# Dividing the softmax probabilities of a local-attention kernel on two engines instead of one

## The chip, the cores and the metric

One core of a Trainium2 chip. The metric is the device time of one execution in microseconds (us). Engines are named TensorE (PE in the profile, PEld for its weight loads), VectorE (DVE), ScalarE (ACT), GpSimd (POOL) and SyncE (SP, which only issues transfers).

## The reference, cut to what matters

The input x has shape (4, 2048, 256), float32. First comes a full self-attention without weights over each sequence of 2048 rows, then two layers of a transformer block, with layer norms and residuals around both parts. The change lies in the two layers. Each layer computes, per row, queries, keys and values for 8 heads of 64, normalises and rotates queries and keys, and attends within windows of 128 rows to the own window and the one before:

```python
sim = jnp.einsum('bhwid,bhwjd->bhwij', bq, bk)      # 128 x 256 for each head and window
sim = jnp.where(mask, -jnp.finfo(sim.dtype).max, sim)
attn = jax.nn.softmax(sim, axis=-1)                 # exp(sim - max) / row sum
out = jnp.einsum('bhwij,bhwjd->bhwid', attn, bv)
...
x = x + o @ wo
h = shift_token(x)                                  # then layer norm
h = h @ w1 + b1
a, g = jnp.split(h, 2, axis=-1)
h = a * jax.nn.gelu(g, approximate=False)
x = x + h @ w2 + b2
```

The division by the row sum in `softmax` is the operation that the change moves.

## The kernel before, in words

The program has a first part (`phase_a`, the unweighted attention, up to some 790 us), a preparation of the weights, and the second part (`phase_b`, both layers, from some 820 us to the end). Only the second part is touched.

**Slots.** The second part is a hand-written software pipeline over 128 windows (64 for each layer) of 128 rows. `slots` (lines 481 to 497) calls a function `run(s, r, pairs, layer)` once for each slot s, with r = s % 4; every engine has its own `run`, and each engine works through its own list in the written order, held only by semaphores. In slot s the projections of window s are made, the attention of window s - 1 up to the probabilities, the rest of the attention of window s - 2, and the layer norm of window s - 3. The feed-forward part works on pairs of windows: its first product (w1) and the gelus come at the end of the even slots (r = 0 and 2), its second product (w2) in the odd slots (r = 1 and 3). So there are 64 slots of each kind that hold attention work. The first 8 slots of each layer are written out; the others run in a loop (`Fori`) with four slots to a turn, and the last slots are written out again. `t` in the code is the window that a block of lines treats.

**The softmax, and who does what around it.** For window t = s - 1, in slot s:

- TensorE makes the scores of a pair of heads p (lines 909 to 915), four pairs, into four PSUM banks.
- VectorE adds the mask, scales, and keeps each head's 128 x 256 scores in SBUF in `probs`, with the negated maximum in `negmax` (line 1160).
- ScalarE takes the exponential in place and gives the row sum (line 1021), eight instructions; then `keep_hT` copies the transposed input of the next window out of PSUM (line 971, to `hT_hi`).
- VectorE, in `normalise(p)` (lines 1166 to 1173), waits for the exponentials of the pair, takes the reciprocal of the two row sums (line 1170, `rinv`) and multiplies both heads' probabilities by it in place (line 1173). Between the pairs stand two other steps: `normalise(0)`, `normalise(1)`, the residual add (line 1184), `normalise(2)`, `keep_hT` (line 1047, the low part `hT_lo`, which waits for ScalarE's `hT_hi`), `normalise(3)` (lines 1175 to 1188).
- In the next slot TensorE transposes the probabilities (line 886) after a wait on `probs_ready`, and ScalarE copies them out of PSUM (line 1009).

**What stands behind it on the two queues.** On VectorE: in odd slots of layer 1 the output norm (line 1105), in even slots six instructions `hid` (line 1196), each after its gelu; then the next slot begins with the low parts of the queries and keys (lines 1120 and 1123, `qT_lo`, `kT_lo`), which wait for ScalarE's `qT_hi` and `kT_hi`. On ScalarE: in even slots a table load and six gelus (line 1036), each into one of two buffers `gl`, so that the third waits for the first `hid` and so on; then the next slot begins with the copies of queries and keys out of PSUM (lines 987, 991, 994), the squares (998, 1000), the values (1003), the transposed probabilities (1009), the attention output (1012), and `h2T` (979) ahead of the next exponentials. On TensorE: in the odd slot behind an even one the transposes of the keys (line 855) wait for the third `hid` (line 853), since they write to the same bank, the projections (line 870) for the first two, and the projection of the values for `qT_lo` (line 863); the transposes of the probabilities (line 886) in even slots wait for the add of line 1084 on VectorE (`xpp_ready`, line 878).

```python
normalise(0)
normalise(1)
...
nc.vector.tensor_tensor(xp[:, r % 2, :], ps[:, 2, 0:D], xr[:, r % 2, :], ALU.add).then_inc(xp_ready, 1)
normalise(2)
if in_range(s + 1):
    keep_hT(s + 1)
normalise(3)
```

Of the kernel before, what the change touches and what calls it, by code (L numbers as in the profile page):

```python
# [21 lines left out]
ALU = mybir.AluOpType  # L22
ACT = mybir.ActivationFunctionType
# [9 lines left out]
LAYERS, HEADS, DH = 2, 8, 64  # L33
INNER = HEADS * DH
HP = HEADS // 2
# [28 lines left out]
def wait(eng, sem, count):  # L64

    if not (isinstance(count, int) and count <= 0):
        eng.wait_ge(sem, count)
# [408 lines left out]
def in_range(t):  # L476

    return not isinstance(t, int) or 0 <= t < NT
# [21 lines left out]
def phase_b(nc, w, consts, x2_dram, xs_dram, xp_dram, rot_dram, out):  # L500
# [9 lines left out]
    with ExitStack() as keep:  # L510
        def sb(name, shape, dt=F32):
            return keep.enter_context(nc.sbuf_tensor("b_" + name, shape, dt))
# [16 lines left out]
        with ExitStack() as ctx:  # L529
# [3 lines left out]
            def sem(name):  # L533
                return ctx.enter_context(nc.semaphore("p_" + name))
# [148 lines left out]
        with ExitStack() as ctx:  # L683
# [22 lines left out]
            probs = sb("probs", [P, HEADS, 2 * P])  # L706
            rowsum, rinv = sb("rowsum", [P, HEADS]), sb("rinv", [P, HEADS])
# [28 lines left out]
            kT_both = sem("kT_both")  # L736
            scores_done, mask_ready = sem("scores_done"), sem("mask_ready")
            scores_kept, exp_done = sem("scores_kept"), sem("exp_done")
            rinv_ready, probs_ready = sem("rinv_ready"), sem("probs_ready")
            pT_done, pT_kept = sem("pT_done"), sem("pT_kept")  # L740
            pv_done, oT_hi, oT_lo, wo_done, xp_ready, xb_ready = (sem(n) for n in ("pv_done", "oT_hi", "oT_lo", "wo_done", "xp_ready", "xb_ready"))
            st2_ready, mv2_ready, var2_ready, rstd2_ready = (sem(n) for n in ("st2_ready", "mv2_ready", "var2_ready", "rstd2_ready"))
# [75 lines left out]
            def _(pe):  # L818
# [21 lines left out]
                def run(s, r, pairs, layer):  # L840
                    t = s - 1
# [32 lines left out]
                    t = s - 2  # L874
                    if in_range(t):

                        if r % 2 == 0:
                            wait(pe, xpp_ready, s - 4)
                        else:
                            wait(pe, hid_ready, HC * (pairs - 1))  # L880
                        for p in range(HP):
                            if p == HP - 1 and in_range(s - 1):
                                pe.wait_ge(kT_lo, 2 * s)
                            pe.wait_ge(probs_ready, HEADS * t + 2 * p + 2)
                            for n in range(4):
                                last = nc.tensor.transpose(ps[:, 3 + p, n * P:(n + 1) * P],  # L886
                                                           probs[:, 2 * p + n // 2, (n % 2) * P:(n % 2 + 1) * P], ident_f[:])
                            last.then_inc(pT_done, 1)

                        pe.wait_ge(v_kept, t + 1)  # L890
                        if not in_range(s):
                            pe.wait_ge(h2T_kept, s - 3)
                        for p in range(HP):
                            pe.wait_ge(pT_kept, HP * t + p + 1)
                            for c in range(2):
                                window = (r - 2 - (r + c) % 2) % 4
                                for h in range(2):
                                    last = nc.tensor.matmul(ps[h * DH:(h + 1) * DH, 7, p * P:(p + 1) * P],  # L898
                                                            v[:, window, (2 * p + h) * DH:(2 * p + h + 1) * DH],
                                                            probsT[:, p, (2 * h + c) * P:(2 * h + c + 1) * P],  # L900
                                                            start=(c == 0), stop=(c == 1))
                        last.then_inc(pv_done, 1)
                    t = s - 1
# [13 lines left out]
                    t = s - 2  # L917
# [44 lines left out]

                transpose_hx(0, 0)
                slots(pe, run)

            @block.scalar
            def _(act):
                def keep_hT(t):
                    act.wait_ge(hT_done, t + 1)
                    wait(act, k_done, t)  # L970
                    nc.scalar.copy(hT_hi[:], ps[:, 7, 0:D].rearrange("p (k n) -> p k n", k=KD)).then_inc(hT_hi_kept, 1)
# [9 lines left out]
                def run(s, r, pairs, layer):  # L981
                    t = s - 1
# [21 lines left out]
                    t = s - 2  # L1004
# [8 lines left out]
                    t = s - 1  # L1013
# [10 lines left out]
                        keep_h2T(s - 3, r, pairs)  # L1024
                    if in_range(s + 1):
                        keep_hT(s + 1)
                    j = pairs - 2
                    if r % 2 == 0 and in_range(2 * j):
                        for c, bank in enumerate(W1_BANKS):
# [9 lines left out]
                keep_hT(0)  # L1039
                act.wait_ge(vk_cleared, 4)  # L1040
                slots(act, run)

            @block.vector
            def _(dve):
# [68 lines left out]
                def run(s, r, pairs, layer):  # L1113
                    t = s - 1
# [11 lines left out]
                    t = s - 3  # L1126
# [9 lines left out]
                    t = s - 3  # L1136
# [10 lines left out]
                    t = s - 1  # L1147
# [18 lines left out]
                    def normalise(p):  # L1166
                        t = s - 1
                        if in_range(t):
                            dve.wait_ge(exp_done, HEADS * t + 2 * p + 2)
                            nc.vector.reciprocal(rinv[:, 2 * p:2 * p + 2], rowsum[:, 2 * p:2 * p + 2]).then_inc(rinv_ready, 1)  # L1170
                            dve.wait_ge(rinv_ready, HP * t + p + 1)
                            for h in range(2 * p, 2 * p + 2):
                                nc.vector.tensor_scalar(probs[:, h, :], probs[:, h, :], rinv[:, h:h + 1], None, ALU.mult).then_inc(probs_ready, 1)  # L1173

                    normalise(0)
                    normalise(1)
                    t = s - 2
                    if in_range(t):
# [4 lines left out]
                        wait(dve, xb_ready, t - 1)  # L1183
# [4 lines that stand above are left out]
# [82 lines left out]
def build(nc, x, wqkv, q_scale, k_scale, wo, ln_g, ln_b, w1, b1, w2, b2, ident, rot, mask, out):  # L1270
    x2_dram = nc.dram_tensor("x2_dram", [NW * P, D], F32).ap()
    xs_dram = nc.dram_tensor("xs_dram", [STREAM_BLOCKS * P, D], F32).ap()
    xp_dram = nc.dram_tensor("xp_dram", [STREAM_BLOCKS * P, D], F32).ap()
    rot_dram = nc.dram_tensor("rot_dram", [P, LAYERS * WPB, 4 * DH], F32).ap()
    phase_a(nc, x, ident, x2_dram, xs_dram, xp_dram)
    weights = dict(wqkv=wqkv, q_scale=q_scale, k_scale=k_scale, wo=wo, ln_g=ln_g, ln_b=ln_b, w1=w1, b1=b1, w2=w2, b2=b2)
    phase_b(nc, weights, dict(ident=ident, rot=rot, mask=mask), x2_dram, xs_dram, xp_dram, rot_dram, out)
# [49 lines left out]
```

## Time and profile before

| | us |
|---|---|
| median of 3 runs | 3440.58 (3440.16 to 3442.09) |
| span of the profiled execution | 3440.9 |
| VectorE busy | 2975.0 (86%) |
| ScalarE busy | 2315.4 (67%) |
| TensorE matmul busy | 3200.0 (93%) |
| GpSimd busy | 1876.9 (55%) |

The span of the profiled execution runs from its first to its last instruction; no other time of that execution is given, and the span lies 0.3 above the median of the runs. Busy shares are means over the whole span; the rows that are quoted further down come from single slots. A row of a view in order of time gives the start in us from the span's start, the length in us, the engine, the line, the operation and how often it stands there in a row; in brackets the idle time ahead of it and who ended it.

### The profile page before, as it was taken

Reading aid. Unit: us, or ns where it says so; the run is one execution under the profiler, and the core shown is the slowest. Engines: PE = TensorE matmul, PEld = TensorE weight load, DVE = VectorE, ACT = ScalarE, POOL = GpSimd, SP = SyncE. Lnnn points to the kernel's source line nnn. Section 1 sums busy time; section 2 is a strip of 40 time slices with the busy share of each in tenths; the row PEclk is TensorE's granted clock in tenths of the full one; section 3 lists DMA queues with packets and bytes.
Section 4 is the critical chain, followed back from the end, with each engine's and each line's share of the span. In section 5 each row is a group of like instructions: output and inputs, shape, how many; then the busy total and the mean of one; then the engine's idle time right before and its main releaser. Section 6 shows DMA issues by size and latency. Waiting matters only on the chain.

```text
span 3440.9 us, 85961 instructions
## 1 busy us (share of the span) xinstructions
PE 3200.0 (93%) x24600; PEld 2670.4 (78%) x24600; DVE 2975.0 (86%) x8121; ACT 2315.4 (67%) x5021; POOL 1876.9 (55%) x2307
## 2 busy tenths in 40 slices
PE   6999999973999999999999999999999999999997
PEld 3666667672888888888888888888888888888886
DVE  6888787857899989988989989998998999899995
ACT  5435353503787777777777777877777777777774
POOL 2433333335665655655655656666665566666662
PEclk9999999985999999999999999999999999999999
DMA  1111111134111111111111111111111111111111
GB/s 35 46 52 41 56 37 55 40 119 140 35 43 40 37 40 41 41 41 41 37 40 45 37 45 38 41 55 43 43 45 46 46 43 43 44 45 51 46 45 36
DMA packets 205536, 163.08 MB, mean 47 GB/s; under 512 B 25646, under 2 KB 203282, under 8 KB 204946
## 3 DMA queue, kind: packets, MB, share of 16 engines
q1 hardware_dynamic: 205330, 161.06, 15.3%
q14 instruction: 166, 1.36, 0.1%
q8 instruction: 40, 0.66, 0.1%
HBM read 106.44 MB, written 54.54 MB: 47 GB/s over the span
## 4 chain that ended last, share of the span: by engine, by line
DVE 24%; issue 18%; PE 18%; ACT 12%; POOL 1%; DVEq 1%; ACTq 1%; DMA 0%; SPq 0%; POOLq 0%
PE b_ps L898 4%; DVE b_probs L1173 4%; PE b_ps L948 3%; ACT b_probs L1021 3%; PE b_ps L870 2%; DVE b_kT_low L1123 2%; DVE b_probs L1160 2%; ACT b_gl L1036 2%; ACT L1021 2%; PE b_ps L886 2%; DVE b_qT L1120 2%; PE b_ps L913 2%; PE b_ps L914 2%; DVE b_t L1062 2%; ACT b_qT L987 2%
## 5 line engine op out<-in xcount | busy, mean ns | idle before, releaser
L870 PE MATMUL b_ps<-b_wqkv,b_hT_hi 128*128 128x512 f32 x1536 | 503.4, 409 | 43.2 <-DVE b_qT L1120 42.2
L1222 POOL TENSOR_TENSOR b_rstd<-b_var,b_mhalf 128x1 f32<-128x1 f32 x128 | 72.2, 564 | 821.1 <-DVE b_var L1134 821.1
L1021 ACT ACTIVATE b_probs<-b_probs,b_negmax 128x256 f32<-128x256 f32 x1024 | 505.6, 495 | 5.7 <-DVE b_negmax L1160 3.3
L948 PE MATMUL b_ps<-b_h2T,b_w 128*128 128x256 f16 x4224 | 474.2, 273 | 0.7 <-ACT b_h2T L979 0.7
L948 PEld LDWEIGHTS b_ps<-b_h2T,b_w 128*128 128x128 f16 x4224 | 414.5, 98 | 49.3 <-ACT b_h2T L979 0.9
L1212 POOL TENSOR_TENSOR b_sq<-b_sq 128x512 f32<-128x512 f32 (+5 forms) x768 | 418.1, 544 | 58.2 <-ACT b_sq L1000 17.9
L1173 DVE TENSOR_SCALAR b_probs<-b_probs,b_rinv 128x256 f32<-128x256 f32 x1024 | 424.8, 456 | 18.1
L1244 POOL TENSOR_TENSOR b_rn<-b_ss_min,b_mhalf 128x16 f32<-128x16 f32 x128 | 379.2, 2963 | 34.9 <-DVE b_ss_min L1071 33.3
L870 PEld LDWEIGHTS b_ps<-b_wqkv,b_hT_hi 128*128 128x128 f32 x1536 | 281.0, 193 | 114.8 <-DVE b_qT L1120 57.8
L442 PE MATMUL a_ps<-a_xs,a_E 128*128 128x256 f16 x3072 | 345.2, 273 | 4.1 <-POOL a_xs L233 4.0
L959 PE MATMUL b_ps<-b_w,b_hid 128*128 128x256 f32 x1536 | 342.2, 379 | 1.2 <-DVE b_hid L1196 1.2
L434 PE MATMUL a_ps<-a_xnT 128*128 128x512 f16 x1536 | 338.0, 384 | 3.0 <-ACT a_xnT L382 2.4
L442 PEld LDWEIGHTS a_ps<-a_xs,a_E 128*128 (+1 forms) x3072 | 297.8, 98 | 40.0 <-issue 6.6
L1160 DVE CUSTOM_DVE_ANT_0 b_probs<-b_ps,b_mask,b_rn 128x256 f32<-128x256 f32 x768 | 323.6, 474 | 0.0
L959 PEld LDWEIGHTS b_ps<-b_w,b_hid 128*128 128x128 f32 x1536 | 286.8, 190 | 37.9 <-DVE b_hid L1196 1.5
L870 PE MATMUL b_ps<-b_wqkv,b_hT_lo 128*128 128x512 f32 x768 | 307.2, 400 | 0.0
L434 PEld LDWEIGHTS a_ps<-a_xnT 128*128 x1536 | 151.3, 99 | 188.5 <-issue 11.5
L1009 ACT COPY b_probsT<-b_ps 128x512 f32<-128x512 f32 x512 | 266.0, 619 | 26.8 <-PE b_ps L886 26.4
L886 PEld LDWEIGHTS b_ps<-b_ident_f,b_probs 128*128 128x128 f32 x2048 | 233.9, 144 | 56.3 <-DVE b_xpp L1084 23.1
L898 PE MATMUL b_ps<-b_probsT,b_v 128*64 128x128 f32 x4096 | 261.0, 280 | 17.2 <-ACT b_probsT L1009 17.1
L886 PE MATMUL b_ps<-b_ident_f,b_probs 128*128 128x128 f32 x2048 | 253.9, 278 | 24.9 <-DVE b_xpp L1084 23.5
L898 PEld LDWEIGHTS b_ps<-b_probsT,b_v 128*64 128x64 f32 x4096 | 217.5, 136 | 55.4 <-ACT b_probsT L1009 36.6
(136 smaller groups left out, 7305.4 us busy)
## 6 DMA issues: line engine op xcount, KB each, us to landing
b_hx<-xs_dram SPq DMA_DIRECT2D x256, 64.0 KB, 1.9
b_rot<-rot_dram SPq DMA_DIRECT2D x128, 128.0 KB, 2.1
b_xr<-xs_dram SPq DMA_DIRECT2D x128, 128.0 KB, 2.1
xp_dram<-b_xp SPq DMA_DIRECT2D x128, 128.0 KB, 1.7
b_h<-xp_dram SPq DMA_DIRECT2D x256, 64.0 KB, 1.8
a_xn<-in_L_attn_x_dram SPq DMA_DIRECT2D x20, 512.0 KB, 3.8
a_x_res<-in_L_attn_x_dram SPq DMA_DIRECT2D x66, 128.0 KB, 2.1
x_dram<-a_x SPq DMA_DIRECT2D x64, 128.0 KB, 1.7
```

What stands on the lines that cost most here:

```text
L434: last = nc.tensor.matmul(ps[:, 4 * u + n, :], xnT[:, a, k, rows], xnT[:, c, k, n * 512:(n + 1) * 512], start=(k == 0 and a == 0 and c == ...
L442: last = nc.tensor.matmul(ps[:, bank, 0:D], E[:, a, j, ds(i * P, P)], xs[:, c, j, :], start=(j == 0 and a == 0 and c == 0), stop=(j == WPB ...
L870: last = nc.tensor.matmul(ps[:, bank, :], hT[:, k, :], wqkv[:, ds(layer(s), 1), part, k, bank * INNER:(bank + 1) * INNER], start=(k == 0 a ...
L886: last = nc.tensor.transpose(ps[:, 3 + p, n * P:(n + 1) * P], probs[:, 2 * p + n // 2, (n % 2) * P:(n % 2 + 1) * P], ident_f[:])
L898: last = nc.tensor.matmul(ps[h * DH:(h + 1) * DH, 7, p * P:(p + 1) * P], v[:, window, (2 * p + h) * DH:(2 * p + h + 1) * DH], probsT[:, p, ...
L948: last = nc.tensor.matmul(ps[:, bank, half * 2 * P:(half + 1) * 2 * P], w1[:, ds(layer(2 * j), 1), wp, k, first:first + P], h2T[:, hp, k, ...
L959: last = nc.tensor.matmul(ps[:, 3, n * D:(n + 1) * D], hid[:, c, n * P:(n + 1) * P], w2[:, ds(layer(2 * j), 1), c, :], start=(c == 0), sto ...
L1021: nc.scalar.activation(probs[:, h, :], probs[:, h, :], ACT.Exp, bias=negmax[:, h:h + 1], scale=-1.0, accum_out=rowsum[:, h:h + 1]).then_in ...
L1160: nc.vector.tensor_tensor_reduce(probs[:, h, :], ps[:, 3 + p, (h % 2) * 2 * P:(h % 2 + 1) * 2 * P], which, rn[:, (r - 1) % 2, h:h + 1], AB ...
L1173: nc.vector.tensor_scalar(probs[:, h, :], probs[:, h, :], rinv[:, h:h + 1], None, ALU.mult).then_inc(probs_ready, 1)
L1212: nc.gpsimd.tensor_tensor(target, target, sq[:, :, width:2 * width], ALU.add).then_inc(ss_halved, 1)
L1244: nc.gpsimd.tensor_tensor(rn[:, r % 2, :], ss_min[:], mhalf[:], ALU.pow).then_inc(rn_ready, 1)
```

## The change

The reciprocals of all four pairs stay on VectorE. The multiplications of pairs 0 and 1 stay there too; those of pairs 2 and 3, four instructions in each slot, become ScalarE activations with the function Copy and the reciprocal as a per-partition scale, placed behind `keep_hT` and ahead of the gelus. TensorE waits for the first two pairs on `probs_ready` and for the other two on a new semaphore `probs_divided`.

```diff
-            rinv_ready, probs_ready = sem("rinv_ready"), sem("probs_ready")
+            rinv_ready, probs_ready, probs_divided = sem("rinv_ready"), sem("probs_ready"), sem("probs_divided")
...
-                            pe.wait_ge(probs_ready, HEADS * t + 2 * p + 2)
+                            if p < HP // 2:
+                                pe.wait_ge(probs_ready, HEADS // 2 * t + 2 * p + 2)
+                            else:
+                                pe.wait_ge(probs_divided, HEADS // 2 * t + 2 * p + 2 - HEADS // 2)
...
                     if in_range(s + 1):
                         keep_hT(s + 1)
+                    t = s - 1
+                    if in_range(t):
+                        for p in range(HP // 2, HP):
+                            act.wait_ge(rinv_ready, HP * t + p + 1)
+                            for h in range(2 * p, 2 * p + 2):
+                                nc.scalar.activation(probs[:, h, :], probs[:, h, :], ACT.Copy, scale=rinv[:, h:h + 1]).then_inc(probs_divided, 1)
                     j = pairs - 2
                     if r % 2 == 0 and in_range(2 * j):
...
-                            for h in range(2 * p, 2 * p + 2):
-                                nc.vector.tensor_scalar(probs[:, h, :], probs[:, h, :], rinv[:, h:h + 1], None, ALU.mult).then_inc(probs_ready, 1)
+                            if p < HP // 2:
+                                for h in range(2 * p, 2 * p + 2):
+                                    nc.vector.tensor_scalar(probs[:, h, :], probs[:, h, :], rinv[:, h:h + 1], None, ALU.mult).then_inc(probs_ready, 1)
```

## Rows read from the trace of the kernel before

**Rows 1.** the page: busy us (share of the span) of each engine
```profile
PE 3200.0 (93%) x24600; PEld 2670.4 (78%) x24600; DVE 2975.0 (86%) x8121; ACT 2315.4 (67%) x5021; POOL 1876.9 (55%) x2307
```

**Rows 2.** slot r = 2, layer 0: window; length; busy PE, PEld, DVE, ACT, POOL; clock; DMA
```profile
1170.22:1190.89 20.67, 20.67 (x179) 18.46 (x179) 19.32 (x55) 16.87 (x40) 11.63 (x13) 1.00 0.19 59
```

**Rows 3.** ScalarE in order of time, end of slot r = 2, layer 0
```profile
1184.70 0.35 ACT L971 CAST b_hT_hi<-b_ps 128x256 fp32r<-128x256 f32 x1
1185.07 1.28 ACT L1036 ACT_TABLE_LOAD   x1
1186.36 1.02 ACT L1036 ACTIVATE b_gl<-b_ps,b_b,b_w_unit 128x256 f32<-128x256 f32 x2
...
1190.28 1.19 ACT L987 CAST b_qT<-b_ps 64x512 fp32r<-64x512 f32 x2
```

**Rows 4.** VectorE in order of time, the same stretch
```profile
1184.79 0.15 DVE L1170 RECIPROCAL b_rinv<-b_rowsum 128x2 f32<-128x2 f32 x1
...
1186.04 1.36 DVE L1173 TENSOR_SCALAR b_probs<-b_probs,b_rinv 128x256 f32<-128x256 f32 x2
1187.31 0.87 DVE L1196 SCALAR_TENSOR_TENSOR b_hid<-b_ps,b_b1a,b_gl 128x256 f32<-128x256 f32 x2
...
1190.89 1.41 DVE L1120 TENSOR_TENSOR b_qT<-b_ps,b_qT 64x512 fp32r<-64x512 f32 x2
```

**Rows 5.** GpSimd in order of time, the same stretch
```profile
1185.46 1.04 POOL L1249 TENSOR_TENSOR b_kr<-b_t,b_rn 128x512 f32<-128x512 f32 x1
```

**Rows 6.** TensorE in order of time, the slot behind it
```profile
1196.09 2.13 PE L898 MATMUL b_ps<-b_probsT,b_v 128*64 128x128 f32 x32 [0.33 <-ACT b_probsT L1009]
```

**Rows 7.** groups by line and shape, ScalarE, whole span: busy us, mean ns
```profile
L1021 ACT ACTIVATE b_probs<-b_probs,b_negmax 128x256 f32<-128x256 f32 x1024 | 505.6, 495 | 5.7 <-DVE b_negmax L1160 3.3
...
L1036 ACT ACTIVATE b_gl<-b_ps,b_b,b_w_unit 128x256 f32<-128x256 f32 x320 | 167.2, 562 | 46.5 <-DVE b_hid L1196 30.6 <-PE b_ps L948 14.0
...
L641 ACT ACTIVATE b_w<-b_w,b_w_unit 128x1536 f32<-128x1536 f32 x2 | 3.0, 1560 | 0.0
```

**Rows 8.** ScalarE in order of time, end of a slot r = 0, layer 1
```profile
2334.21 1.02 ACT L1036 ACTIVATE b_gl<-b_ps,b_b,b_w_unit 128x256 f32<-128x256 f32 x2
...
2337.78 1.19 ACT L987 CAST b_qT<-b_ps 64x512 fp32r<-64x512 f32 x2
```

**Rows 9.** ScalarE in order of time, end of slot r = 1, layer 0
```profile
1168.10 0.35 ACT L971 CAST b_hT_hi<-b_ps 128x256 fp32r<-128x256 f32 x1
1169.56 1.19 ACT L987 CAST b_qT<-b_ps 64x512 fp32r<-64x512 f32 x2 [1.10 <-PE b_ps L848]
```

**Rows 10.** VectorE in order of time, the same stretch
```profile
1167.52 1.62 DVE L1173 TENSOR_SCALAR b_probs<-b_probs,b_rinv 128x256 f32<-128x256 f32 x2
1169.06 0.41 DVE L1047 TENSOR_TENSOR b_hT_lo<-b_ps,b_hT_hi 128x256 fp32r<-128x256 f32 x1
...
1169.58 0.62 DVE L1173 TENSOR_SCALAR b_probs<-b_probs,b_rinv 128x256 f32<-128x256 f32 x2
1170.22 1.41 DVE L1120 TENSOR_TENSOR b_qT<-b_ps,b_qT 64x512 fp32r<-64x512 f32 x2
```

**Rows 11.** ScalarE in order of time, end of an odd slot, layer 1
```profile
2232.38 0.35 ACT L971 CAST b_hT_hi<-b_ps 128x256 fp32r<-128x256 f32 x1
2233.93 1.19 ACT L987 CAST b_qT<-b_ps 64x512 fp32r<-64x512 f32 x2 [1.20 <-PE b_ps L848]
```

**Rows 12.** VectorE in order of time, the same stretch
```profile
2234.44 0.73 DVE L1105 TENSOR_SCALAR b_fin<-b_xpp,b_mvf,b_rstdf 128x256 f32<-128x256 f32 x2
2235.20 1.41 DVE L1120 TENSOR_TENSOR b_qT<-b_ps,b_qT 64x512 fp32r<-64x512 f32 x2
```

**Rows 13.** VectorE in order of time, at a turn of the loop, layer 0, then layer 1
```profile
1211.06 1.41 DVE L1120 TENSOR_TENSOR b_qT<-b_ps,b_qT 64x512 fp32r<-64x512 f32 x2 [2.47 <-issue]
...
2317.01 1.41 DVE L1120 TENSOR_TENSOR b_qT<-b_ps,b_qT 64x512 fp32r<-64x512 f32 x2 [2.42 <-issue]
```

**Rows 14.** waits of VectorE, whole span: us in total, times, longest
```profile
DVE b_qT L1120 <- issue: 61.4, 25, 2.9
```

## The prediction

> **What bounds the kernel now.** I read the page first. VectorE is busy 86% of the span, ScalarE 67% [rows 1], which invites moving work from the one to the other. That share is a mean, so I went on to the instructions in order of time at the ends of single slots. The slot r = 2 of layer 0 shows TensorE with matmuls on record in all of its 20.67 us, VectorE in 19.32, ScalarE in 16.87 [rows 2]: there is no single bound, and what counts is which engine is late where the slots join. The joint is ScalarE's copy of the queries (line 987), on which VectorE's line 1120 waits.
>
> In an **even** slot ScalarE runs from the last exponentials over the copy of line 971, the table load and six gelus to line 987 [rows 3]. Nothing lies idle ahead of the load (1184.70 + 0.35 = 1185.05, load at 1185.07). VectorE takes its first `hid` at 1187.31 [rows 4], although the first gelu ends at about 1186.36 + 0.56 = 1186.92: there VectorE is late, by 0.4. So both queues are close to critical, and ScalarE has 0.35 to spare: from first gelu to line 987 it takes 3.92 here (1186.36 to 1190.28) [rows 3] and 3.57 in the slot whose `hid` come in time [rows 8].
>
> In an **odd** slot ScalarE idles 1.10 to 1.20 ahead of line 987, released by TensorE [rows 9, 11]. VectorE's line 1120 starts 0.66 behind line 987 in layer 0 (1169.56 to 1170.22) [rows 9, 10], just behind the first of its two halves, so VectorE is no later than TensorE. In layer 1 VectorE has the output norm besides and starts 1.27 behind (2233.93 to 2235.20) [rows 11, 12]: there it is the late one.
>
> **The price of a division on ScalarE.** No row shows it at this size. Line 641 is the same operation (Copy, scale from a column, in place) on 1536 columns, 1.560 us; the exponential, with one column operand, takes 0.495 on 256 [rows 7]. The line through both has 0.83 ns a column, so the two are of one kind and a division takes 0.495. Two gelus of 0.562 take 1.02 together [rows 3, 7], so they start 0.46 apart, 0.10 less than their length; divisions then start 0.40 apart. Four push the next instruction back by 1.60 where it may overlap, and by 3 x 0.40 + 0.495 = 1.70 where it does not, as the table load. Bounds: line 971's 0.35 [rows 3], 0.25 apart, and the gelu's 0.562, 0.46 apart. I take 0.40, since line 641 is the very operation.
>
> **Removed on VectorE.** In an odd slot pair 2 takes 1.54 (1167.52 to 1169.06) and pair 3 0.53, together 2.07 [rows 10]. In an even slot pair 3 takes 1.27 (1186.04 to 1187.31) [rows 4], and pair 2, which nothing disturbs there, 0.53: 1.80. The reciprocals stay.
>
> **Even slots, 64.** The reciprocal of pair 2 is ready at 1184.94 [rows 4], before ScalarE is free, and that of pair 3 follows `hT_lo` at about 1185.6; no wait. The divisions start at 1185.07, the load moves by 1.71 to 1186.78, the first gelu to 1188.07. VectorE is now free long before, so from there the 3.57 hold: line 987 at 1191.64 instead of 1190.28, 1.36 later, and line 1120 with it. VectorE's 1.80 turn into waiting for the first gelu. Where the 3.57 hold already, in the slots r = 0 behind a turn of layer 1's loop (12), it is the full 1.71. Sum 52 x 1.36 + 12 x 1.71 = 91.2. It is not made good in the odd slot: TensorE waits there for the third `hid`, and 0.33 for ScalarE's copy of the probabilities [rows 6], so the delay passes on to the next exponentials.
>
> **Odd slots.** Layer 0: the divisions start at 1168.10 + 0.37 = 1168.47, line 987 can start at 1170.07, against 1169.56 [rows 9]: 0.51 later, line 1120 too, VectorE's 2.07 worth nothing. VectorE's reciprocal of pair 3 is ready at about 1168.97 (`hT_lo` needs line 971, 1168.45, then 0.34 and 0.15), before the third division. There are 32 such slots, 13 of them ahead of a turn of the loop; 19 x 0.51 = 9.7. Layer 1: line 987 at 2232.75 + 1.60 = 2234.35, line 1120 some 0.61 behind, at 2234.96 instead of 2235.20 [rows 11, 12]; VectorE would be ready at 2234.05. 20 x (-0.24) = -4.8.
>
> **Turns of the loop, 25** [rows 14], 13 in layer 0 and 12 in layer 1. Ahead of line 1120 VectorE stands for 2.47 or 2.42 without a releaser [rows 13]; I take it for the cost of the jump back. It starts when VectorE's last instruction is through, and that one ends 1.2 earlier (1170.20 to 1168.97 in the measure of rows 10; in layer 1 1.15). If ScalarE pays nothing at its own jump, the gain is -1.2 and -1.15. If it pays as VectorE does behind its last division, layer 0 has 1168.47 + 1.70 + 2.47 + 0.61 = 1173.25 against 1172.69, +0.56, and layer 1 -0.1. No row shows ScalarE's jump on its own, since TensorE holds it back at that place. I take the middle: 13 x (-0.3) - 12 x 0.65 = -12; ends -29 and +6.
>
> **The sum.** 91.2 + 9.7 - 4.8 - 12 = 84 us. The span is 3440.9 and the median 3440.58, so both are one base: 3440.6 + 84 = 3525.
>
> **Semaphores and queues.** No transfer moves. ScalarE's new wait stands ahead of gelus and of line 987; it is met each time, as shown, because the reciprocals stay in VectorE's order ahead of `hid`. TensorE's wait for `probs_divided` comes late in the next slot, over 4 us behind the last division.
>
> **The rivals.**
> *VectorE is the bound (faster).* Its place is VectorE's queue between line 1170 and line 1120. If ScalarE's divisions fell into idle time, each pair of slots would lose 1.80 + 2.07 = 3.87, or 64 x 3.87 = 248 in all: 3193. For it: the 86%; and pair 3 takes 1.36 instead of 0.62 while GpSimd works on SBUF (1185.46 for 1.04) [rows 4, 5]. Against: no idle time of ScalarE between line 971 and the gelus [rows 3]. It decides as soon as the gelus can slip by 1.36 without moving line 987. The Trainium skill's Perfetto Trace Analysis, section Optimizing Scalar/DVE Operations, says that with VectorE saturated it may pay to give work to ScalarE, and that VectorE and GpSimd share a port; by that rule this rival holds. The slowed pair agrees with the port, the missing idle time speaks against the rule here.
> *Cheap divisions.* At 0.25 apart each slot has 0.60 less: even slots 91.2 - 38.4 = 53, odd slots of layer 0 nothing, of layer 1 20 x (-0.66) = -13 (TensorE then holds line 987 at 2233.93), turns -29: +11, 3451.
> *Dear divisions, or a slower clock.* At 0.46 apart each slot has 0.24 more: 91.2 + 15.4 + 9.7 + 4.6 + 13 x 0.80 + 1 = 132, 3573. TensorE also waits about 1 us more in each even slot; its granted clock is 1.00 there [rows 2], the 2.4 GHz level, and if it fell at times, the time would be in this region too.
> *The freed time of the odd slots and turns just cancels the even ones:* needs both low ends and more; within 0.2%.
>
> The Trainium skill's ScalarE: Activation LUTs, section Rules for kernel authors, wants multiplications on VectorE and not on ScalarE. The undisturbed pair of 0.62 on VectorE [rows 10] against 0.40 + 0.495 for a pair on ScalarE agrees with it.
>
> **Chances and range.** Forecast 0.74; VectorE bound 0.06; cheap 0.07; dear or slower clock 0.10; cancelled 0.03. A measurement of this kernel can tell about 0.2%, some 7 us, from no change. Only the first rival is faster, only the last is within 0.2%: faster 0.06, same 0.03, slower 0.91. The forecast's own ends are the turns' (3508 and 3543), and half the way to the cheap and dear prices widens them to 3475 and 3570, which leaves out less than 2 in 10.
>
> **What would show it.** In the changed profile: four Copy instructions of 0.49 in each slot, 0.40 apart, 512 in all; in even slots the table load 1.7 later behind line 971, VectorE idle some 2.6 us ahead of its first `hid`, released by the gelu, and 3.57 from first gelu to line 987; in odd slots no idle time of ScalarE ahead of line 987; VectorE's busy share down by some 240 us of work, ScalarE's up by 250. At the turns, an idle time of ScalarE ahead of line 987 without a releaser, or none, settles that term. Wrong would be: a gap between line 971 and the first division (the reciprocal late), line 987 of the even slots less than 1 us later, or TensorE's clock below 1.00 in layer 0.

## The result, and the profile after

| | us |
|---|---|
| before, 4 runs | 3441.04 median (3440.16 to 3442.09) |
| after, 4 runs | 3486.75 median (3484.45 to 3490.2) |
| ratio | 1.0134, 95% interval 1.0120 to 1.0148 |
| span of the profiled execution after | 3484.5 |

The kernel is slower, by 46 us: on the side that the prediction gave, inside its range of 3475 to 3570, and 38 us short of its +84.

The page of after, busy us of each engine (before: [rows 1]):

```profile
PE 3208.2 (92%) x24600; PEld 2657.2 (76%) x24600; DVE 2734.9 (78%) x7609; ACT 2510.3 (72%) x5533; POOL 1868.4 (54%) x2307
```

VectorE's busy time fell by 240 us, ScalarE's rose by 195 (not by 250 as predicted: 512 divisions of 0.499 are 255, but busy time counts an overlap of neighbours once: the row below has 218.3 for them), and TensorE's stayed. The time rose all the same.

Groups by line and shape, ScalarE in after: busy us, mean ns, idle time ahead of them and its releasers. The divisions are line 1035; lines 971, 987, 1036, 1047, 1120, 1170, 1173 and 1196 of before are now 974, 990, 1045, 1056, 1129, 1179, 1183 and 1206.

```profile
L1024 ACT ACTIVATE b_probs<-b_probs,b_negmax 128x256 f32<-128x256 f32 x1024 | 505.6, 495 | 5.7 <-DVE b_negmax L1169 3.3
...
L1035 ACT ACTIVATE b_probs<-b_probs,b_rinv 128x256 f32<-128x256 f32 x512 | 218.3, 499 | 1.1 <-DVE b_rinv L1179 1.1
```

There are 512 divisions of 0.499, as long as an exponential (0.495), and they wait 1.1 us in all.

ScalarE in order of time, end of an even slot of layer 0 in after (before: [rows 3]):

```profile
1155.41 0.35 ACT L974 CAST b_hT_hi<-b_ps 128x256 fp32r<-128x256 f32 x1
1155.67 1.71 ACT L1035 ACTIVATE b_probs<-b_probs,b_rinv 128x256 f32<-128x256 f32 x4
1157.39 1.28 ACT L1045 ACT_TABLE_LOAD   x1
1158.69 1.02 ACT L1045 ACTIVATE b_gl<-b_ps,b_b,b_w_unit 128x256 f32<-128x256 f32 x2
...
1162.26 1.19 ACT L990 CAST b_qT<-b_ps 64x512 fp32r<-64x512 f32 x2
```

Four divisions last 1.71, so they stand 0.40 apart. From line 974 to the table load it is 1.98 against 0.37 before, so the load comes 1.61 later; from line 974 to the copy of the queries it is 6.85 against 5.58 [rows 3], so the copy comes 1.27 later. The 3.57 from the first gelu to that copy is what [rows 8] had.

VectorE in order of time at the same place (before: [rows 4]):

```profile
1156.14 0.15 DVE L1179 RECIPROCAL b_rinv<-b_rowsum 128x2 f32<-128x2 f32 x1
1159.29 0.94 DVE L1206 SCALAR_TENSOR_TENSOR b_hid<-b_ps,b_b1a,b_gl 128x256 f32<-128x256 f32 x2 [2.99 <-ACT b_gl L1045]
```

VectorE is through with the slot's softmax at 1156.29 and waits 2.99 us for the first gelu. Its freed time has become waiting.

TensorE's clock in two even slots of layer 0, by window: length; busy PE, PEld, DVE, ACT, POOL; granted clock; DMA (before: [rows 2]):

```profile
1140.20:1162.20 22.00, 19.64 (x171) 16.99 (x170) 17.13 (x50) 17.33 (x41) 11.57 (x13) 1.00 0.19 57
1180.96:1202.94 21.98, 20.75 (x178) 18.19 (x177) 17.60 (x52) 18.57 (x44) 11.56 (x13) 1.00 0.22 66
```

The slot is 1.3 longer at a granted clock of 1.00, the 2.4 GHz level, as before: the clock has no part in what the divisions cost here. It has a part at the turns of layer 1, further down.

ScalarE in order of time, end of an odd slot of layer 0 in after (before: [rows 9]):

```profile
1178.48 0.35 ACT L974 CAST b_hT_hi<-b_ps 128x256 fp32r<-128x256 f32 x1
1178.74 1.71 ACT L1035 ACTIVATE b_probs<-b_probs,b_rinv 128x256 f32<-128x256 f32 x4
1180.35 1.17 ACT L990 CAST b_qT<-b_ps 64x512 fp32r<-64x512 f32 x2
```

Here the idle time ahead of the copy of the queries, 1.10 before, is filled, and 0.41 more: 1.87 from line 974 to it against 1.46.

Waits of after, whole span: us in total, times, longest.

```profile
DVE b_hid L1206 <- ACT b_gl L1045: 232.0, 197, 5.6
...
DVE b_hT_lo L1056 <- ACT b_hT_hi L974: 75.0, 106, 3.7
DVE b_qT L1129 <- ACT b_qT L990: 73.7, 58, 3.1
```

And two waits of before:

```profile
DVE b_hid L1196 <- ACT b_gl L1036: 47.1, 141, 5.6
ACT b_qT L987 <- PE b_ps L848: 72.6, 64, 2.5
```

In after, ScalarE's wait for TensorE at line 990 (line 987 of before) is down from 72.6 us to a single one of 2.5. ScalarE is now the late one at the joints of two slots.

So far it is much as predicted. The difference lies at the **turns of the loop**. VectorE in order of time at a turn of layer 0, then at one of layer 1, in after (before: [rows 13]):

```profile
1219.25 0.15 DVE L1179 RECIPROCAL b_rinv<-b_rowsum 128x2 f32<-128x2 f32 x1
1222.44 1.41 DVE L1129 TENSOR_TENSOR b_qT<-b_ps,b_qT 64x512 fp32r<-64x512 f32 x2 [3.04 <-ACT b_qT L990]
...
2320.11 0.73 DVE L1114 TENSOR_SCALAR b_fin<-b_xpp,b_mvf,b_rstdf 128x256 f32<-128x256 f32 x2 [0.22 <-DVE b_rinv L1179]
2321.47 1.41 DVE L1129 TENSOR_TENSOR b_qT<-b_ps,b_qT 64x512 fp32r<-64x512 f32 x2 [0.62 <-ACT b_qT L990]
```

The first of them names ScalarE's copy as the releaser. ScalarE in order of time at the same turn says otherwise:

```profile
1220.38 1.18 ACT L990 CAST b_qT<-b_ps 64x512 fp32r<-64x512 f32 x2
```

The first half of that copy, which is all that line 1129 needs, ended about 0.6 later, at 1221.0, and VectorE still stood for 1.4 us. The idle time is the stall of the jump back, now mostly hidden behind a wait. In layer 1 the stall is gone altogether: line 1129 starts 0.6 behind ScalarE's copy (line 990 at 2320.87), as inside the loop. Where did it go?

The DMA view of 2300 to 3200 us (layer 1), rows of the queues, has an answer to look into: a queue that carries instructions. Its packets, in before and then in after:

```profile
q14 instruction: 55, 0.45, 0.2%
```

```profile
q14 instruction: 5, 0.04, 0.0%
```

Before has 5 packets of 8 KB to each of its 11 turns in this stretch; in after they are gone but for 5 and 3 others on another queue, all outside of 2400 to 3200. In 1100 to 1900 us (layer 0) both have 50, again 5 to a turn.

The whole account by kind of slot follows. A slot's length is taken from one copy of the queries on ScalarE to the next in order of time; each figure is the mean over the loop's rounds (14 in layer 0, 13 in layer 1), and r = 0 is the slot that begins a round. The first round is entered without a jump back, so there are 13 and 12 jumps, the turns that the prediction counts. "Shifted" kernels are explained with their experiments.

| kernel | layer 0: r = 0, 1, 2, 3 | layer 1: r = 0, 1, 2, 3 |
|---|---|---|
| before | 23.07, 17.68, 20.71, 17.67 | 23.83, 18.29, 21.41, 18.29 |
| after | 23.47, 18.08, 21.98, 18.08 | 21.98, 18.71, 21.98, 18.70 |
| even slots only | 24.26, 17.67, 22.03, 17.68 | 25.64, 18.30, 22.76, 18.30 |
| odd slots only | 22.09, 18.08, 20.81, 18.08 | 23.80, 18.69, 20.63, 18.70 |
| behind the gelus | 23.63, 17.95, 22.08, 17.95 | 22.09, 18.71, 22.09, 18.69 |
| after, shifted | 21.99, 18.08, 21.98, 18.08 | 21.97, 18.69, 21.97, 18.69 |
| before, shifted | 20.68, 17.67, 20.69, 17.68 | 21.40, 18.32, 21.41, 18.29 |
| before, shifted less | 20.68, 17.69, 20.69, 17.68 | 23.69, 18.31, 21.40, 18.29 |
| after, stalling in layer 1 | 23.48, 18.09, 21.99, 18.09 | 23.70, 18.70, 21.98, 18.70 |
| odd, pair 2 alone, shifted | 20.65, 17.68, 20.65, 17.67 | 20.78, 18.33, 20.77, 18.29 |
| odd, pairs 2 and 3, shifted | 20.64, 18.08, 20.64, 18.09 | 20.63, 18.81, 20.64, 18.69 |
| even, pair 3 alone, shifted | 22.26, 17.68, 22.22, 17.66 | 22.96, 18.33, 22.96, 18.30 |
| even, pair 2 alone, shifted | 21.22, 17.69, 21.20, 17.68 | 21.95, 18.33, 21.95, 18.29 |

Both r = 0 and r = 2 are even slots, so their difference is what a turn costs, as a mean over all rounds: before 2.36 in layer 0 and 2.42 in layer 1, after 1.49 and nothing. In us: before 14 x 2.36 + 13 x 2.42 = 65, after 14 x 1.49 = 21. The turns gave back 44.

In layer 1 a part of this is TensorE's clock. Two turns of before and one of after, from one copy of the queries to the next (columns as above):

```profile
2313.24:2337.78 24.54, 22.27 (x178) 19.25 (x177) 19.99 (x59) 17.32 (x40) 13.23 (x15) 0.93 0.20 59
2560.33:2583.87 23.54, 21.17 (x180) 18.37 (x179) 20.14 (x59) 17.12 (x39) 13.26 (x15) 1.00 0.20 60
```

```profile
2361.51:2383.47 21.96, 20.71 (x178) 18.17 (x177) 17.11 (x50) 18.56 (x44) 13.21 (x15) 1.00 0.24 71
```

In before, 8 of the 12 slots behind a jump in layer 1 have a granted clock of 0.93 on average; they last 24.26 us, the other four 23.60. In after all are at 1.00. So some 8 x 0.66 = 5 of the 31 us that the turns of layer 1 cost before go with the clock. In this loop of before every slot without a jump ahead of it is at 1.00.

### The profile page after: what moved, and what is told of

It reads as the page before. It is cut to its first block, busy times and chain, and to the rows that moved or that the text cites. A ratio compares the mean times of both kernels' runs of the same rounds, so it can differ in the third digit from the quotient of the medians.

```text
span 3484.5 us, 85882 instructions
## 1 busy us (share of the span) xinstructions
PE 3208.2 (92%) x24600; PEld 2657.2 (76%) x24600; DVE 2734.9 (78%) x7609; ACT 2510.3 (72%) x5533; POOL 1868.4 (54%) x2307
## 4 chain that ended last, share of the span: by engine, by line
ACT 27%; PE 20%; issue 15%; DVE 12%; POOL 1%; ACTq 1%; DVEq 0%; DMA 0%; POOLq 0%; SPq 0%
ACT b_probs L1024 10%; PE b_ps L901 6%; ACT b_probs L1035 4%; PE b_ps L889 4%; PE b_ps L916 3%; ACT b_gl L1045 3%; PE b_ps L917 3%; DVE b_kT_low L1132 2%; ACT b_qT L990 2%; ACT L1045 2%; PE b_ps L962 2%; DVE b_qT L1129 2%; DVE b_hid L1206 2%; ACT L1024 2%; DVE b_xpp L1093 1%
## 5 line engine op out<-in xcount | busy, mean ns | idle before, releaser
L1206 DVE SCALAR_TENSOR_TENSOR b_hid<-b_ps,b_b1a,b_gl 128x256 f32<-128x256 f32 (+1 forms) x384 | 181.2, 482 | 238.4 <-ACT b_gl L1045 232.0
L382 ACT COPY a_xnT<-a_ps 128x512 f16 x80 | 46.1, 587 | 310.3 <-PE a_ps L412 310.2
```

## The experiments

The theory: the divisions move ScalarE's copy of the queries back in each even slot, VectorE's freed time is worthless, and the turns of the loop gave back more than predicted. Rivals: the even slots cost less than their 1.3, or the loss comes from TensorE's wait for the third `hid` (it waits 56.0 us there in all in after) and not from ScalarE's queue.

### The move in one kind of slot alone

A pair that a list `ON_ACT` names is divided by ScalarE, the others by VectorE; its first entry is for odd slots, its second for even ones. It is `((), (2, 3))` in the kernel with the move in even slots only and `((2, 3), ())` in the other. TensorE's counts on the two semaphores follow it.

```diff
+ON_ACT = ((), (2, 3))
...
-                        for p in range(HP // 2, HP):
+                        for p in ON_ACT[(r - 1) % 2]:
...
-                            if p < HP // 2:
+                            if p not in ON_ACT[(r - 1) % 2]:
                                 for h in range(2 * p, 2 * p + 2):
```

Even slots only:

> Divisions of pairs 2 and 3 on ScalarE in even slots alone; odd slots as in the kernel before. Theory (ScalarE's queue sets the joint behind the gelus): from one copy of the queries on ScalarE to the next, even slots not behind a turn of the loop take about 1.25 us more than before in both layers (20.70 to 21.95 in layer 0, 21.40 to about 22.65 in layer 1), odd slots stay at 17.68 and 18.29, the stalls of VectorE at the turns stay; 64 x 1.25 = 80, time about 3521. Rival (VectorE is the bound, the divisions are hidden): no slot longer, time under 3441.

Measured: 3536.48 (3533.13 to 3539.87), ratio 1.0284 (1.0266 to 1.0301), +97. The even slots r = 2 rose by 1.32 in layer 0 and 1.35 in layer 1 (table), where 1.36 was predicted, and the odd ones stayed. The slots and turns of the table make 86 + 3 of the 97; the four runs spread over 7 us, and the profiled one, 3533.13, is the lowest. The turns cost 2.88 in layer 1 (before 2.42) and 2.23 in layer 0 (before 2.36); the wait of this kernel, whose line 1137 is line 1120 of before:

```profile
DVE b_qT L1137 <- issue: 68.7, 25, 3.2
```

Odd slots only:

> Divisions of pairs 2 and 3 on ScalarE in odd slots alone; even slots as before. Theory: odd slots of layer 0 take 0.41 more (18.09), a pair of slots in layer 1 about 0.24 less (39.69 to 39.45), and at the turns VectorE reaches its stall earlier, 0.6 to 0.9 each; in sum 19 x 0.41 - 13 x 0.6 - 20 x 0.24 - 12 x 0.9 = -16, time about 3425. Rival (the odd slots pay as the even ones do): 3441 + 64 x 0.41 = 3467.

Measured: 3441.34, ratio 1.0006 (0.9996 to 1.0015). The odd slots of both layers rose by 0.41; in layer 1 the even slot behind them got 0.78 shorter, since VectorE's output norm no longer ends late, so a pair gained 0.37. In layer 0 the turn costs 22.09 - 20.81 = 1.28 instead of 2.36, in layer 1 it costs 3.17 instead of 2.42: the turns were expected to give 19 us and gave 14 x 1.08 - 13 x 0.75 = 5. The slots missed too: all 32 odd slots of layer 0 pay their 0.41, not only the 19 that were counted, and its even slots rose by 0.10. That is +16 where 8 were expected, against -12 in layer 1 where -5 were expected.

Why a turn of layer 1 costs more in this kernel shows in part. From VectorE's last reciprocal to its first instruction behind the jump it is 4.69 there on average, against 3.77 before (4.51 with even slots only), and in 10 of the 12 slots behind the jump the granted clock is 0.93 or lower. In both kernels of this section VectorE's loop of layer 1 begins some 24 instructions earlier than before. Whether that place makes the stall longer was not tested.

### The divisions behind the gelus

```diff
-                    t = s - 1
-                    if in_range(t):
-                        for p in range(HP // 2, HP):
...
                     j = pairs - 2
                     if r % 2 == 0 and in_range(2 * j):
...
+                    t = s - 1
+                    if in_range(t):
+                        for p in range(HP // 2, HP):
...
```

> As the changed kernel, but in even slots the four divisions stand behind the six gelus. Theory (what counts is ScalarE's work ahead of its copy of the queries, wherever it stands): gelus and hid come 1.7 earlier, the copy of the queries at the same place, time within 10 us of the changed kernel's 3487. Rival (what costs is TensorE's wait for the third hid, 56 us in all, which goes away here): 3430 or less.

Measured: 3486.31, ratio 1.0131 (1.0114 to 1.0148), as after. ScalarE in order of time at the end of an even slot of this kernel:

```profile
1156.38 1.02 ACT L1039 ACTIVATE b_gl<-b_ps,b_b,b_w_unit 128x256 f32<-128x256 f32 x2
...
1159.95 1.71 ACT L1046 ACTIVATE b_probs<-b_probs,b_rinv 128x256 f32<-128x256 f32 x4
1161.68 1.19 ACT L990 CAST b_qT<-b_ps 64x512 fp32r<-64x512 f32 x2
```

The gelus, and with them the `hid`, come early again: no wait of TensorE for the third `hid` is left in this kernel's waits, and the kernel is no faster. So it is not the wait for `hid`: the four divisions cost the same on either side of the gelus, as work on ScalarE ahead of its copy of the queries.

### The code moved, the work left alone

The last question is whether the stall hangs on where the code lies. VectorE got instructions that only raise a semaphore nobody waits for, 70 of them ahead of the first slot and 58 spread over the first 8 slots of layer 1, so both loops keep their bodies and start later in VectorE's instruction stream.

```diff
+                for _ in range(70):
+                    dve.sem_inc(passed_dve, 1)
                 keep_hT(0)
                 slots(dve, run)
```

After, shifted (70 and 58):

> As the changed kernel, with 70 semaphore instructions put on VectorE's queue ahead of its slots and 58 between the two loops, so that both loop bodies begin elsewhere in the code. Theory (the stall at a turn is a refetch of code that depends on whether the loop body, 323 and 351 instructions, lies in three or in four blocks of 128 instructions, 8 KB): the 3.05 us of VectorE ahead of its first instruction at the turns of layer 0 goes, no instruction packets in either loop, 13 x 1.6 = 21 us less and some 5 us for the added instructions, time about 3470. Rival (the stall follows from what VectorE waits for, not from the place of the code): layer 0 keeps its stalls, 3487 to 3492.

Measured: 3467.48, ratio to before 1.0081 (1.0065 to 1.0098), 19 us below after. Its r = 0 slots are as long as r = 2 in both layers (table), and the rows of the queues for 1100 to 1900 us have none that carries instructions.

Before, shifted (50 and 28), and shifted less (50 and 10):

> The kernel before, with 50 semaphore instructions on VectorE's queue ahead of its slots and 28 between the loops; the divisions all stay on VectorE. Theory (a turn stalls when the loop body lies in four blocks of 128 instructions): the bodies of 337 and 365 instructions then begin where three blocks hold them, surely in layer 0 and in two cases of three in layer 1. Layer 0 loses 2.47 a turn, 13 x 2.45 = 32 less: 3408; with layer 1 too, 12 x 3.1 = 37 more: 3371. Some 3 us for the added instructions. Rival (the stall belongs to the order of VectorE's work): 3440.

> As before_shift with 10 instead of 28 instructions between the loops, for the other third of the places that layer 1's loop may have. Theory: one of the two has no instruction packets in either loop and takes about 3374, the other only keeps layer 1's stalls and takes about 3410 (both may be free of them). Rival: 3440.

Measured: 3381.01 (3377.94 to 3381.91), ratio 0.9827 (0.9811 to 0.9844), and 3405.94, ratio 0.9902 (0.9885 to 0.9918). With no change to its work the kernel is 59 us faster. Shifted by 18 instructions less in layer 1, only layer 1 stalls (r = 0 is 23.69 there), and the wait and the packets are back; the wait over the whole span (line 1122 is line 1120 of before), and the queue in 2300 to 3200 us, of the kernel shifted less:

```profile
DVE b_qT L1122 <- issue: 27.1, 12, 2.5
```

```profile
q14 instruction: 55, 0.45, 0.2%
```

After, stalling in layer 1 (0 and 50):

> The changed kernel with 50 semaphore instructions on VectorE between the two loops, so that layer 1's loop begins 47 instructions later, about where it began before the change. Theory (the change moved the loop out of the stall by its place in the code): the refetch is back in layer 1, with 1.6 to 2.3 us more a turn, 12 turns, and some 3 us for the added instructions: 3509 to 3518, which is what the change costs when both kernels stall. Rival (fewer instructions on VectorE, or its waiting, removed the stall): 3487 to 3490.

Measured: 3509.94, ratio 1.0206 (1.0189 to 1.0223), 23 above after; r = 0 in layer 1 is 23.70 again, and the queue in 2300 to 3200 us has

```profile
q14 instruction: 57, 0.47, 0.2%
```

So the price of the change at equal placement is 3467.48 - 3381.01 = +86 where neither kernel stalls and 3509.94 - 3439.96 = +70 where both do in both layers; it is less there because after hides a part of its stalls (23.48 - 21.99 = 1.49 and 23.70 - 21.98 = 1.72 a turn, against 2.36 and 2.42). The +46 of the kernels as given is a mixture: one that stalls in both layers against one that stalls in one.

### Fewer divisions, where there is room

Pair 2 alone in odd slots (two divisions, some 0.8 us, into 1.1 of idle time), and pairs 2 and 3 there, both shifted free of stalls (55 and 36; 60 and 44), `ON_ACT = ((2,), ())` and `((2, 3), ())`:

> Only pair 2 in odd slots goes to ScalarE, everything else stays on VectorE; both loops placed as in before_shift (55 and 36 semaphore instructions), so no stalls at the turns. To be held against before_shift, 3381. Theory: two divisions (0.9) fit into ScalarE's 1.1 of idle time, so layer 0 is as before (20.70 and 17.68), and in layer 1, where VectorE is the late one at this joint, each pair of slots is shorter by about 0.6 (39.70 to 39.1): 3381 - 32 x 0.62 = 3361. Rival (ScalarE loses its slack at this joint too): 3381 or more.

> Pairs 2 and 3 of odd slots on ScalarE, even slots on VectorE, loops placed free of stalls (60 and 44 instructions). Theory: four divisions (1.6) don't fit into 1.1: layer 0's odd slots 18.08 instead of 17.68, a pair of slots in layer 1 39.3 instead of 39.7; 32 x 0.5 - 32 x 0.38 = +4 against before_shift: about 3385. Rival (four divisions free VectorE more, so more is gained than with two): under 3361.

Measured: 3361.71 (3359.71 to 3365.04), ratio 0.9774 (0.9757 to 0.979), and 3381.25, ratio 0.9829 (0.9812 to 0.9845). ScalarE in order of time at the end of an odd slot of the first of them:

```profile
1167.02 0.35 ACT L982 CAST b_hT_hi<-b_ps 128x256 fp32r<-128x256 f32 x1
1167.27 0.90 ACT L1043 ACTIVATE b_probs<-b_probs,b_rinv 128x256 f32<-128x256 f32 x2
1168.38 1.19 ACT L998 CAST b_qT<-b_ps 64x512 fp32r<-64x512 f32 x2 [0.21 <-PE b_ps L858]
```

The two divisions fit, TensorE still releases the copy, and layer 1 gains 0.63 a pair of slots: 32 x 0.63 = 20, the 19 us below the shifted before. This version is faster than both kernels of the change: 59 of the 78 us against the kernel before are the placement, 19 the divisions. All four divisions fill the idle time and 0.41 more, which takes the gain away again (3381.25 against 3381.01).

The same for one pair in even slots, `((), (3,))` and `((), (2,))`, both shifted by 56 and 36:

> Only pair 3 of even slots on ScalarE, loops placed free of stalls (56 and 36 instructions). Theory (each division pushes the gelus by 0.40, 0.35 of it is covered by the lateness of VectorE, which pair 3 ends): 0.82 - 0.35 = about 0.47 an even slot, 64 x 0.47 = 30: 3411. Rival (cost in proportion, half of the 1.27 that four divisions cost): 64 x 0.64 = 41: 3422. Rival (VectorE's slowed pair 3 is what an even slot waits for): 3381 or less.

> Only pair 2 of even slots on ScalarE, loops placed free of stalls (56 and 36 instructions), to be held against before_shift (3381) and even_pair3_shift (3481). In the latter ScalarE waited 0.96 in each even slot for the reciprocal of pair 3. Theory: pair 2's reciprocal is ready before ScalarE is free, so no wait; two divisions push the load by 0.82, 0.35 of it is covered: 64 x 0.47 = 30, about 3411, and the difference of some 70 to even_pair3_shift is that wait. Rival (any division between the exponentials and the gelus costs about 1.3 to 1.5 a slot, whatever is waited for): 3465 to 3481.

Measured: 3481.16, ratio 1.0121 (1.0104 to 1.0138), a miss by 70 us, and 3415.88, ratio 0.9934 (0.9917 to 0.995), 5 above what was expected. What the first one missed is a wait, 60.1 us in its 64 even slots; in order of time on ScalarE:

```profile
1114.21 0.35 ACT L982 CAST b_hT_hi<-b_ps 128x256 fp32r<-128x256 f32 x1
1115.52 0.91 ACT L1043 ACTIVATE b_probs<-b_probs,b_rinv 128x256 f32<-128x256 f32 x2 [0.96 <-DVE b_rinv L1189]
1116.44 1.28 ACT L1053 ACT_TABLE_LOAD   x1
```

and on VectorE:

```profile
1114.27 0.15 DVE L1189 RECIPROCAL b_rinv<-b_rowsum 128x2 f32<-128x2 f32 x1
1114.46 0.61 DVE L1193 TENSOR_SCALAR b_probs<-b_probs,b_rinv 128x256 f32<-128x256 f32 x2
1114.99 0.41 DVE L1064 TENSOR_TENSOR b_hT_lo<-b_ps,b_hT_hi 128x256 fp32r<-128x256 f32 x1
1115.33 0.15 DVE L1189 RECIPROCAL b_rinv<-b_rowsum 128x2 f32<-128x2 f32 x1
```

The reciprocal of pair 3 stands behind VectorE's division of pair 2 and `hT_lo`, so ScalarE waits for it in each even slot, 0.96 here. With pair 2 moved instead, its reciprocal is there in time, this wait is 0.5 us in all, and two divisions cost 3415.88 - 3381.01 = 35 us, or 35 / 64 = 0.54 a slot. The 65 us between the two kernels are that wait, to within 6. The change itself moves both pairs: VectorE then has no division ahead of the second reciprocal, and ScalarE does the first pair meanwhile.

## Why the prediction was right in kind and off in size

- **The bound.** It was read from the joint of two slots and not from the busy shares, and that held. ScalarE has no room ahead of its copy of the queries in even slots (0.35 us by the prediction), and the kernel with the move in even slots alone is 97 us slower, turns included. The rival "VectorE is the bound" is refuted by the time, and by the 2.99 that VectorE now waits for the gelu.
- **The price of a division.** 0.495 and 0.40 apart were taken from line 641 and the exponential; 0.499 and 0.40 were measured. The cheap and the dear rivals fall with it.
- **Even slots.** 1.36 later was predicted; 1.27 in after, and 1.32 and 1.35 where they were changed alone. Of the 0.1 in layer 0, part is that the first division begins 0.26 behind line 974 and not 0.37, since it may overlap its end; the table load had moved by 1.61, not 1.71.
- **Odd slots.** +0.51 in layer 0 was measured as +0.41: there too the first division begins 0.26 behind line 974. The -0.24 a pair in layer 1 was -0.37 where they were changed alone. It shows up in the next slot: the odd slots themselves got longer in both layers.
- **Slots in sum.** The prediction had 91.2 + 9.7 - 4.8 = +96 without the turns; the kernels free of stalls differ by +86. A pair of slots was put at 1.36 + 0.51 = 1.87 in layer 0 and at 1.36 - 0.24 = 1.12 in layer 1; by the rows of the two shifted kernels it is 1.29 + 0.40 = 1.69 and 0.57 + 0.39 = 0.96. Over 32 pairs each that is 6 + 5 us, the whole of this difference.
- **The turns of the loop: the step that failed.** -12 was predicted, with ends of -29 and +6; the turns gave -44. Nearly all of the miss is in layer 1. Counted as in the table, with every slot at its full price, the prediction had 13 x (-0.3 - 0.51) = -10.5 for layer 0 and 12 x (-0.65 + 0.24 + 0.35) = -0.7 for layer 1; measured are -12 and -31. Two things were wrong in it. The stall was taken for a fixed cost of each jump, counted from the end of VectorE's last instruction. First, in layer 0 it lasts 3.19 us from line 1179 at 1219.25 to line 1129 at 1222.44, and before it was the same counted from the last reciprocal, 0.15 + 0.53 for the two divisions + 2.47 = 3.15. So it begins where VectorE's last wait is passed and not where its last instruction ends: taking the two divisions away does not bring its end forward, as the low end of this term had it, but ScalarE's later copy hides more of it, 14 x (2.36 - 1.49) = 12 us. ScalarE pays nothing at its own turns (r = 3, ahead of a jump, is as long as r = 1). That start is read from the traces: over the 13 jumps the mean time from the last reciprocal to that line is 3.38 in before and 3.27 with even slots only, where the divisions ahead of the jump stay on VectorE, and 3.33 in after and 3.30 with odd slots only, where they are gone. No kernel was made to test it alone. That the term came out so near in layer 0 is luck: it was the middle between two guesses, of which one took the wrong start and the other a jump of ScalarE that costs nothing here. Second, it is no fixed cost at all. The change makes the loop of layer 1 on VectorE shorter (351 instructions for 365) and moves it forward by 50, and the 13 rounds lost their 2.42: 31 us, some 5 of them the clock's. The kernels with added instructions show that this comes from placement, and that it can be had without the change.
- **The range.** 3487 lies below the forecast's own ends (3508 to 3543). It lies inside the range only by the margin that was added for cheap divisions, and the divisions were not cheap. (Half the way from those ends to 3451 and 3573 is 3480 and 3558, not the 3475 and 3570 that were given; the measured time lies in both.)

The sums agree: +86 for the slots less 44 for the turns is +42, against +46 measured. Some us stay between them. One source is a single stall at the start of the second part, 5.0 in the shifted before and 6.8 in the shifted after, each in place of a wait of 3.7.

The prediction cited the Trainium skill's Perfetto Trace Analysis, section Optimizing Scalar/DVE Operations, for giving work to ScalarE where VectorE is saturated. The runs agree with it only as far as the receiving queue had idle time at that place: pair 2 in odd slots made the kernel 19 us faster, four divisions in even slots made it 97 slower, the turns included.

## What to carry to other kernels

Before work is moved to a less busy engine, look in order of time at the place where it lands and count the idle time ahead of the first instruction there that others wait for: the place with 1.1 us idle took two divisions (0.90) and not four (1.71), and in the place with 0.35 us to spare two divisions left a delay of 0.54. Check in the same view what the moved step's input stands behind on the giving engine; one reciprocal behind two other steps cost some 1.0 us a slot (65 us over 64). And when idle time without a releaser stands at every turn of a loop, treat it as movable: compare kernels only at like placement of the code, and try a shift of the loop before anything else.

## What the runs showed of the hardware that was not expected

A jump back of VectorE's loop costs 2.2 to 3.2 us here, or nothing, by where the loop lies (1.3 to 1.7 where a wait hides a part). The sign is an idle time with "issue" as its releaser, or one put down to a wait that was long over, together with rows of a queue that carries instructions, 5 packets of 8 KB to a turn. The table has positions and sizes in VectorE instructions. The sizes and the distances between the starts can be counted in the traces, which record VectorE's register, branch and semaphore instructions too, and agree within one; only the zero of the count, 796 for before, is from the compiled program.

```
kernel                 layer 0: start, body   stalls   layer 1: start, body   stalls
before                      796, 337          yes          1664, 365          yes
after                       780, 323          yes          1614, 351          no
even slots only             788, 331          yes          1639, 359          yes
odd slots only              787, 329          yes          1640, 357          yes
after, stalling             780, 323          yes          1661, 351          yes
after, shifted              850, 323          no           1739, 351          no
before, shifted less        846, 337          no           1724, 365          yes
before, shifted             846, 337          no           1742, 365          no
odd, pair 2, shifted        847, 333          no           1743, 361          no
```

The kernel with the divisions behind the gelus has the positions of after. The other three shifted kernels begin at 847 or 848 and at 1740 to 1744 and are free.

A reading that fits every line: code is held in blocks of 128 instructions, and a body stalls where it spans four of them (with an offset of 53 to 67 instructions between this count and the blocks). If any block size is tried, stalls and free loops are told apart only by blocks of 127 to 133 (free at three) and of 226 to 235 (free at two), so blocks of 256 are ruled out. The reading was used to choose the shifts. They came out as it said; for the two shifts of before it left open which would be free in layer 1. How many blocks are kept, and why TensorE's loop, which is longer (some 180 matmuls in a slot), shows no such stall stay open. The added instructions cost no time that could be measured apart from their effect on the stall.
